# First layer of a graph network on turned node tiles, centred by means that go through DRAM

## What is computed

```
h = max(layernorm(x), 0)                      # no gain, no shift
def sage(x, Wp, bp, Wl, bl, Wr):
    p   = relu(x @ Wp.T + bp)
    agg = segment_sum(p[src], dst) / max(count(dst), 1)
    return agg @ Wl.T + bl + x @ Wr.T
def relu_ln(x, g, b):                          # relu, then layernorm with g and b
    ...
h = relu_ln(sage(h, layer 0), g0, be0)
h = relu_ln(sage(h, layer 1), g1, be1)
out = x + sage(h, layer 2)
```

## Time and profile before

| | us |
|---|---|
| median of 3 runs | 1519.19 |
| lowest and highest | 1514.76, 1520.58 |
| the profiled execution | 1518.14 |
| its span in the profile | 1516.4 |

### The profile page before, as it was taken

The page is one execution under the profiler, slowest core; times in us unless marked ns, Lnnn a source line. Parts: engine busy times, 40 slices in busy tenths (PEclk is TensorE's granted clock), DMA queues, the critical chain, the costliest instruction groups (busy, mean ns, idle before and its releaser), DMA issues.

```text
span 1516.4 us, 21038 instructions
## 1 busy us (share of the span) xinstructions
PE 1493.8 (99%) x7213; PEld 1216.6 (80%) x7213; DVE 970.3 (64%) x2084; ACT 682.8 (45%) x1267; POOL 604.6 (40%) x532
## 2 busy tenths in 40 slices
PE   7999999999999999999999999999999999999999
PEld 5788887888888888888788888888888777888887
DVE  7999875555555686766565555568766746555552
ACT  5545552332233676766223233356666732233221
POOL 4774355666523000100434432334464463444221
PEclk9999999999999999999999999999999999999999
DMA  8899875555544778786654555479999984554545
GB/s 304 313 347 318 287 260 181 119 85 91 95 85 56 257 268 306 266 284 241 197 111 85 91 91 90 54 249 343 381 349 356 367 279 95 91 90 84 94 59 146
DMA packets 157734, 298.14 MB, mean 197 GB/s; under 512 B 21565, under 2 KB 21756, under 8 KB 157500
## 3 DMA queue, kind: packets, MB, share of 16 engines
q1 hardware_dynamic: 127308, 231.17, 43.6%
q0 software_dynamic: 29744, 64.57, 24.7%
q10 hardware_dynamic: 576, 1.05, 0.2%
HBM read 136.54 MB, written 160.08 MB: 196 GB/s over the span
## 4 chain that ended last, share of the span: by engine, by line
PE 85%; DMA 5%; DVE 3%; issue 3%; POOL 2%; ACT 1%; SPq 1%; ACTq 0%; POOLq 0%
PE bank L750 11%; PE bank L751 11%; PE bank L752 11%; PE bank L738 9%; PE bank L842 7%; PE bank L840 7%; PE bank L841 7%; PE bank L821 7%; PE bank L820 7%; PE bank L819 7%; DMA residual<-x 3%; DMA node_x<-xn 1%; POOL residual L627 1%; DMA rows_in<-node_z 1%; ACT xn L957 1%
## 5 line engine op out<-in xcount | busy, mean ns | idle before, releaser
L750 PE MATMUL bank<-w_high,h_low 128*128 128x512 f32 x876 | 365.8, 418 | 0.0
L751 PE MATMUL bank<-w_low,h_high 128*128 128x512 f32 x876 | 346.6, 396 | 0.0
L752 PE MATMUL bank<-w_high,h_high 128*128 128x512 f32 x876 | 345.8, 395 | 0.0
L977 ACT ACTIVATE h_high<-h_pre 128x500 fp32r<-128x500 f32 x120 | 74.7, 622 | 448.9 <-DVE h_pre L1272 448.9
L609 POOL DMA_INDIRECT rows_in<-node_x,sorted_src x120 | 123.9, 1032 | 247.3 <-PE bank L738 169.3
L752 PEld LDWEIGHTS bank<-w_high,h_high 128*128 128x128 f32 x876 | 165.8, 189 | 39.9
L819 PE MATMUL bank<-xt_low,w_high 128*128 128x500 f32 x480 | 195.2, 407 | 1.7 <-issue 1.7
L957 ACT ACTIVATE xn<-rows_in,off,rstd 128x512 f32<-128x512 f32 x237 | 188.4, 804 | 15.0 <-issue 12.5
L840 PE MATMUL bank<-w_high,h_low 128*125 128x512 f32 x480 | 190.6, 397 | 1.0 <-DVE h_low L1278 1.0
L842 PE MATMUL bank<-w_high,h_high 128*125 128x512 f32 x480 | 190.0, 396 | 0.0
L751 PEld LDWEIGHTS bank<-w_low,h_high 128*128 128x128 f32 x876 | 165.9, 189 | 29.7
(11 more groups left out here) (114 smaller groups left out, 2251.1 us busy)
## 6 DMA issues: line engine op xcount, KB each, us to landing
node_x<-xn SPq DMA_DIRECT2D x237, 256.0 KB
rows_in<-node_z SPq DMA_DIRECT2D x158, 256.0 KB
node_z<-rows_out SPq DMA_DIRECT2D x142, 256.0 KB
out<-rows_out SPq DMA_DIRECT2D x79, 256.0 KB, 4.0
rows_in<-x SPq DMA_DIRECT2D x78, 256.0 KB
residual<-x SPq DMA_DIRECT2D x78, 256.0 KB, 5.0
rows_in<-node_x SPq DMA_DIRECT2D x24, 256.0 KB, 2.6
node_z<-bias_z SPq DMA_DIRECT2D x16, 256.0 KB
```

The source lines that it names most:

```text
L750: nc.tensor.matmul(psum, low[:, k, :], w_high("r", l)[:, k, :], start=(k == 0), stop=False)
L751: nc.tensor.matmul(psum, high[:, k, :], w_low("r", l)[:, k, :], start=False, stop=False)
L752: last = nc.tensor.matmul(psum, high[:, k, :], w_high("r", l)[:, k, :], start=False, stop=(k == K - 1))
```

## The change

Only layer 0 and the start of its edge stage are changed.

- **Turned loads.** The host gives x a second time as `x_t`, in which every node tile lies turned (feature by node). SyncE loads a tile of it straight into `xn` (ring of 4, 5 steps ahead of the product). The four transposes of each node tile are gone, and so is the store to `node_x` of layer 0.
- **Means.** In a turned tile a node is a column, so the mean must lie along the columns on every partition. For product tiles below 20 and for the late tiles ScalarE and VectorE write a diagonal of minus the means in a high and a low part (128x128), and TensorE multiplies both by ones (`spread_mean`, two matmuls of 128x128). From tile 20 on, the means of four tiles (`minus_mean`, 16 bytes on a partition) are stored to DRAM and loaded back to all partitions (2 KB each).
- **Centring.** VectorE adds them to the turned tile, in place (`centre`, 128x512). ScalarE writes the high part with relu from it, VectorE the low part. Both read SBUF where they read PSUM before. The tile is not divided.
- **Roots.** ScalarE keeps the root of each node (`spread`), VectorE inverts four tiles at once, and `node_out` of layer 0 multiplies by it while it adds the bias. `late_out` does so for late tiles.
- **Statistics** of a product tile stand 5 to 6 steps ahead at first, then two tiles in a step from step 3 to step 9, then 12 steps ahead, so that they end at step 58 (before, they ended later).
- **Edges.** Edge rows are gathered from x itself, so they are normalised after the gather: for each of 40 edge tiles `bn_stats`, `bn_aggr`, root, `rstd`, `off` and a ScalarE pass in place, from step 63 on and then beside the edge stage.
- **Ranks** are made by ScalarE (sign with a sum) in place of VectorE, and `rows_of` has one operation more. `edges_in_order` moves from step 54 to 58. GpSimd gathers the first 8 edge tiles before it spreads `carry`, and 12 columns of counts instead of 16 before the ninth tile. The counts stand 2.5 to a step from step 5, instead of 2 from step 3.
- At the end of layer 0 the late tiles get their means after each edge product, and layers 1 and 2 wait for the low part of the last late tile before they load rows.

```diff
+STATS = ((2, 6), (8, 5), (22, None), (None, 12))
+AHEAD_DIAG = 4
+AHEAD_SPREAD = 3
+AHEAD_SPLIT = 2
+BY_PE = 20
+EARLY = 2
+AHEAD_LOAD_T = 5
+DIAGS = 3
...
+COUNTS = 5
...
+STEP_COUNTED = 21
+STEP_SORTED = 58
+EARLY_COUNTS = 12
...
+STEP_EDGE_NORM = 63
...
+            def load_turned(t):
+                slot = t % XN_RING
+                if t >= XN_RING:
+                    sp.wait_ge(xt_low_done, node_no(0, t - XN_RING) + 1)
+                sp.dma_start(xn[:, slot, :], x_t[t * P:(t + 1) * P, :]).then_inc(t_loaded[slot], DMA)
...
+                    if l == 0 and XN_RING <= i + AHEAD_LOAD_T < product_count[0]:
+                        load_turned(i + AHEAD_LOAD_T)
+                    for g in means_at(i - 1) if l == 0 else ():
+                        sp.wait_ge(n_minus, unit_of[0][min(4 * g + 3, product_count[0] - 1)] + 1)
+                        sp.dma_start(mean_table[g], minus_mean[:, 4 * g:4 * g + 4]).then_inc(mean_stored, DMA)
+                    for g in means_at(i - 2) if l == 0 else ():
+                        sp.wait_ge(mean_stored, DMA * (g - BY_PE // 4 + 1))
+                        sp.wait_ge(rows_stored, DMA)
+                        if g - BY_PE // 4 >= 2:
+                            sp.wait_ge(n_centred, 4 * (g - 1))
+                        sp.dma_start(mean_rows[g % 2].rearrange("p m a -> p (m a)"),
+                                     mean_table[g:g + 1].rearrange("g p a -> g (p a)").to_broadcast([P, 4 * P])
+                                     ).then_inc(mean_loaded[g % 2], DMA)
...
+                    out=rows_in[:, slot, :], out_offset=None, in_=node_x if l else x_in,
...
+                    if l == 0 and t == IN_RING:
+                        spread_carry()
+                        pool.wait_ge(count_rows, 1)
+                        pool.wait_ge(counts_stored, DMA)
+                        for c in range(EARLY_COUNTS):
+                            gather_counts(c)
...
+                pe.wait_ge(n_diag_low, d + 1)
+                psum, slot = bank[c % 2][:, 0:P], d % DIAGS
+                nc.tensor.matmul(psum, ones_r[:], diag_low[:, slot, :], start=True, stop=False)
+                nc.tensor.matmul(psum, ones_r[:], diag_high[:, slot, :], start=False, stop=True).then_inc(turned, 1)
...
+            def first_xt_high(t):
+                act.wait_ge(n_centred, t + 1)
+                if t >= XT_RING:
+                    act.wait_ge(n_product, t - XT_RING + 1)
+                S.activation(node_xt(True, t), xn[:, t % XN_RING, :], ACT.Relu).then_inc(xt_high_done, 1)
...
+                S.activation(diag_high[:, slot, :], ident[:], ACT.Identity, scale=minus_mean[:, t:t + 1]
+                             ).then_inc(n_diag_high, 1)
...
+            def node_centre(t):
+                dve.wait_ge(t_loaded[t % XN_RING], DMA * turns(t, XN_RING))
+                if t < BY_PE:
+                    dve.wait_ge(turned, turn_value(node_no(0, t)))
+                    centre(xn[:, t % XN_RING, :], bank[t % 2][:, 0:P])
+                else:
+                    g = t // 4
+                    dve.wait_ge(mean_loaded[g % 2], DMA * ((g - BY_PE // 4) // 2 + 1))
+                    centre(xn[:, t % XN_RING, :], mean_rows[g % 2][:, :, t % 4])
...
+            def centre(rows, minus):
+                x = rows.rearrange("p (k m) -> p k m", k=K)
+                minus = minus.rearrange("p (a m) -> p a m", a=1).to_broadcast([P, K, P])
+                V.tensor_tensor(x, x, minus, ALU.add).then_inc(n_centred, 1)
...
+                    V.scalar_tensor_tensor(out=rows_out[:, slot, :], in0=bank[4 + t % 4][:],
+                                           scalar=spread[:, t:t + 1], in1=bias_z[:], op0=ALU.mult, op1=ALU.add
+                                           ).then_inc(n_out, 1)
...
+                    else:
+                        for u in first_units(i):
+                            first_stats(u)
+                        if is_product(l, i - 1):
+                            node_out(l, i - 1)
+                        for u in first_units(i):
+                            first_mean(u)
+                        for t in first_at(i, AHEAD_SPREAD):
+                            node_centre(t)
+                        for u in first_units(i):
+                            minus_of(u)
+                        for cols in scales_at(i):
+                            scale_of(cols)
+                        for t in first_at(i, AHEAD_SPLIT):
+                            node_xt_low(l, t)
+                        for t in first_at(i, AHEAD_DIAG):
+                            if t < BY_PE:
+                                diag_low_of(t)
+                        for k in R_CHUNKS.get(i, ()):
+                            low_of("r", 0, k)
+                        edge_statistics(edge_norms(i))
                     if l and i in LATE_OUT_AT:
                         late_out(l - 1, LATE - len(LATE_OUT_AT) + LATE_OUT_AT.index(i))
                     if l == 0 and i == STEP_ROWS_FLOAT:
                         keys_along_rows()
...
+                first_norms = range(2 * GROUP, 2 * GROUP + 2) if l == 0 else ()
+                edge_statistics(first_norms)
...
                 h_pre_of(l, 0, 0)
+                edge_factors(first_norms)
```

More of the change, by code:

```diff
@@ L311, in units_at @@
         def units_at(l, p):
-            units = []
-            for n in range(max(0, p - len(LATER)), min(p + 1, product_count[l])):
-                if n + (sum(n < c for c in LATER) if l == 0 else 0) == p:
-                    u = unit_of[l][n]
-                    units += [u] + ([u + 1] if u + 1 < NODE_TILES and tile_of[l][u + 1] >= product_count[l] else [])
-            return units
+            if not 0 <= p < product_count[l]:
+                return []
+            u = unit_of[l][p]
+            return [u] + ([u + 1] if u + 1 < NODE_TILES and tile_of[l][u + 1] >= product_count[l] else [])
@@ new lines, in first_at, with stats_step, stats_at @@
+        def first_at(i, ahead):
+            return [t for t in (i + ahead, i + ahead + 1) if 0 <= t < product_count[0]
+                    and t - ahead - (1 if t < EARLY else 0) == i]
+        def stats_step(t):
+            for until, ahead in STATS:
+                if until is None or t < until:
+                    return t - ahead if ahead else STATS[1][0] - STATS[1][1] + (t - STATS[1][0]) // 2
+        def stats_at(i):
+            return [t for t in range(product_count[0]) if stats_step(t) == i]
@@ new lines, in first_units, with scales_at, means_at @@
+        def first_units(i):
+            return [u for t in stats_at(i) for u in units_at(0, t)]
+        def scales_at(i):
+            last = product_count[0] - 1
+            found = [slice(t - t % 4, t + 1) for t in stats_at(i - 1) if t % 4 == 3 or t == last]
+            return found + ([slice(last + 1, NODE_TILES)] if last in stats_at(i - 1) else [])
+        def means_at(i):
+            last = product_count[0] - 1
+            return [t // 4 for t in stats_at(i) if t >= BY_PE and (t % 4 == 3 or t == last)]
@@ L320, in late_no, with edge_norms_beside, counts_at @@
+        def edge_norms_beside(s):
+            t = s + 2 * GROUP + 3
+            return [t - 1, t] if s == 0 else [t] if t < EDGE_TILES else []
+        def counts_at(i):
+            return [t for t in range(EDGE_TILES) if STEP_COUNT + 2 * t // COUNTS == i]
         def late_no(t):
@@ L879, in _ @@
                     edge_product(l, s)
+                    for j in late_turns(l, s) if l == 0 else ():
+                        late_turn(l, j)
                 if l + 1 < LAYERS:
@@ new lines, in rank @@
+            def rank(t):
+                g = t // GROUP
+                if t == 0:
+                    act.wait_ge(digits, 5)
+                else:
+                    act.wait_ge(placed, t)
+                act.wait_ge(row_loaded[t // (EDGE_TILES // ROW_CHUNKS)], DMA)
+                S.activation(unused[0:EDGE_ROWS, :],
+                             key_row[0:EDGE_ROWS, g * GROUP:(g + 1) * GROUP, :].rearrange("p a e -> p (a e)"),
+                             ACT.Sign, bias=key_f[0:EDGE_ROWS, t:t + 1], scale=-1.0,
+                             accum_out=place[0:EDGE_ROWS, t:t + 1]).then_inc(placed, 1)
@@ L1014, in _ @@
                     edge_xt_high(l, t)
+                for t in range(2 * GROUP, 2 * GROUP + 2) if l == 0 else ():
+                    std_of(t % IN_RING, t)
+                for t in range(2 * GROUP, 2 * GROUP + 2) if l == 0 else ():
+                    edge_norm(t)
                 for m in range(GROUP):
@@ L1059, in late_out, with late_centre, scale_of @@
+            def late_centre(j):
+                c = late_no_of(0, j)
+                dve.wait_ge(late_loaded[j], DMA)
+                dve.wait_ge(turned, turn_value(c))
+                centre(rows_in[:, j, :], bank[c % 2][:, 0:P])
+            def scale_of(cols):
+                dve.wait_ge(n_root, max(unit_of[0][t] for t in range(cols.start, cols.stop)) + 1)
```

(1 more changed line is left out.)

374 lines of the change are left out of this document (254 added, 120 removed).

## The result

The changed kernel takes 1544.37 us (median of 4 runs, 1542.50 to 1547.21), the kernel before on the same chip 1517.38. The ratio is **1.0180** (95% interval 1.0167 to 1.0193): slower by 27 us, and 4 us beyond the upper end of the range. The profiled execution has a span of 1542.8 us against 1516.4.

A forecast was written before the change was run, and what follows sets the result against it. VectorE becomes the bound before step 59; -5.1 us to the first edge product, +0.3 for late tiles and +7.5 for costs bounded from afar make +2.7 on 1518.14: 1521 us, own range 1512 to 1527, 8 in 10 within 1502 to 1540.

The forecast's parts named there:

- The bound: Layer 0's node stage: VectorE, 2.84 us a step on average, becomes the bound above TensorE's 2.80, until step 59.
- what rows bounded only from afar: VectorE before step 59: turned loads 3 us, means through DRAM 1, GpSimd beside VectorE 2, masks and spreads 1.5; together +7.5.
- the centring (two inputs of 512, 0.60 as its neighbours): VectorE's new addition of the means to each turned tile in a node step: 0.60 us, like neighbouring operations.
- rival 3: From tile 20 on, centring reads means at every fourth word: 0.28 us each, 14 us over 51 tiles, 1535; chance 0.13.
- GpSimd beside VectorE: Low part and centring, with two SBUF inputs, slow down beside GpSimd work such as Wl's split: 2 us, ends 0 and 4.
- Loads and means: Late turned loads 3 us for steps 1 to 9 (0 to 15); SyncE's wait for the means' store 1 us (0 to 13).
- Rival 2: Node steps: turned loads' landing sets the step, 15 us more, up to 25 with means' waits; 1530 to 1545; chance 0.22.
- The small operations: VectorE's small operations in a plain node step, among them `minus_mean`: 0.12 and 0.13 us.
- Late tiles: Late tiles lose eight turns (3.4 us), get sixteen short matmuls (1.8 to 3.7) and two waits of about 0.7: +0.3.
- The first steps and the masks: VectorE ends step 9 at 58.3 us; masks and spreads on steps 5 to 20 add 1.5 us, ends 0 and 4.
- Edge rows' statistics hidden: Edge stage: 0.92 us more a tile on VectorE and two ScalarE passes, beside about 6 us of TensorE's work, cost nothing.
- The path to the first edge product: GpSimd's gathers after edges in order at 210.5 us hold VectorE; first edge product at 261.4 us, -5.1 against today.

The follow-up runs named there:

- run 2: Changed kernel, but from tile 20 on the centring reads its means at steps of 1, 2, 3 or 4 words by tile (values wrong): 1542.65 us, single run.
- run 4: Changed kernel with means read at neighbouring words (values wrong) and the four low halves of Wl made by VectorE: 1531.04 us, ratio 1.0089.
- run 5: run 4, but from tile 20 on a turned load brings one row of 128 (values wrong): 1514.91 us, ratio 1.0050.
- run 6: run 4, but the means' load reads weights of the same size, without waiting for the means' store (values wrong): 1523.32 us in a single run, ratio 1.0096.
- run 1: Changed kernel, but from tile 20 on the centring reads its means as 128 neighbouring words (values wrong): 1538.8 us, ratio 1.0139.
- run 3: Changed kernel, but the four low halves of layer 0's Wl are made by VectorE in steps 48 to 51, not GpSimd: 1541.88 us, ratio 1.0165.
- run 7: run 3, but all 71 tiles' means are spread by TensorE, none through DRAM: 1527.38 us, ratio 1.0134.
- run 9: run 3, but means are stored by pairs of tiles, 256 pieces of 8 bytes, and every second word is read: 1551.12 us, ratio 1.0271.
- run 11: run 3 with the strided read, but turned loads of one row instead of 128 from tile 20 on (values wrong): 1529.21 us, ratio 1.0128.
- run 10: run 3, but ScalarE turns each four means into dense rows, and late tiles' diagonals come one edge tile earlier: 1528.25 us, ratio 1.0120.
- run 8: run 4 with true values, means stored turned in 512 pieces of 4 bytes so they come back dense: 1598.18 us, ratio 1.0605.

## Why the prediction was wrong

**The bound** was right: VectorE full, TensorE with gaps. **The sum** was wrong. By the prediction's own stations (step ends on VectorE, us):

| | forecast | measured | excess of the stretch |
|---|---|---|---|
| end of step -1 | 18.0 | 19.7 | +1.7 |
| end of step 9 | 58.3 | 59.6 | -0.4 |
| end of step 20 | 93.3 | 98.5 | +3.9 |
| end of step 58 | 207.2 | 229.8 | +17.4 |
| first edge product | 261.4 | 290.4 | +6.4 |
| from there to the end | 1250.2 | 1252.4 | +2.2 |

The forecast put 7.5 us on top for what rows bounded only from afar; 23.7 us are missing beyond them.

- **The step that failed is "the centring (two inputs of 512, 0.60 as its neighbours)".** With dense means it is 0.58 from start to start, with the table's means 0.97: 51 x 0.37 = 19 us over the forecast, 4 in the third stretch's steps, 38 in the fourth's, 9 in the fifth's. I had seen it and made it rival 3, with a chance of 0.13 and a price of 0.28 us from a difference of 22 ns between two operations of 40 elements. The price was too low (0.28 where it is 0.40), and the chance was far too low: run 2 shows the cost in each of its twelve reads at every fourth word. Rival 3 is what happened. Its time, 1535, was short by the terms below.
- **GpSimd beside VectorE**, 2 us with an end at 4: it was 5.4 in one piece. The earlier trace rows showed one addition of 1.28 us holding one operation; four in a row held one operation for all four, and the TensorE behind it.
- **Loads and means**, 3 + 1 us: 10.8 us of VectorE's waits for turned loads in after. Within the ends given, but elsewhere: 1.3 us in steps 1 to 9, where I had them, and 9.5 from tile 20 on. Rival 2 was true as a mechanism, but masked by the strided read; runs 4 to 6 lay it bare. The means' way through DRAM by itself cost nothing that run 6 could show.
- **The small operations** were taken as 0.12 and 0.13 and are 0.09 and 0.06. In steps 21 to 58 all that is neither centring nor wait takes 85.8 us, where the forecast has 91.1: -5.3, which hid part of the miss. So the stretch's 17.4 us are 14.1 of strided read, 5.4 behind GpSimd and 3.3 of waits for loads, less 5.3.
- **Late tiles**, +0.3: it was 1.3. "Two waits of about 0.7" became three gaps of 0.92 to 1.00 and 2.9 us of idle TensorE, since ScalarE makes the diagonals behind a high half and an edge tile's output in its own order.
- **The first steps and the masks** were right: 0.4 us off over steps 0 to 9.
- **Edge rows' statistics hidden:** right in the edge stage from 307 us on (TensorE 30.00 of 30 us). At its start the wait of 1.06 us for ScalarE's pass is most of 1.2 us that the forecast put at nothing. In steps 63 to 67, where I had TensorE as the bound at 2.80, VectorE needs 3.86 us a step: 5.3 us in five steps, most of the fifth stretch's 6.4.
- **The path to the first edge product** was forecast as GpSimd's chain of gathers, with VectorE waiting for the ninth and tenth edge tile. In after it takes their statistics at 276.85 us without a wait, so VectorE's own work is the path. The forecast's 210.5 us for edges in order also stands 3.3 us behind its own end of step 58 without a reason; in after the first gather starts at 228.63, before that step ends.

What stays open: run 5 has its first edge product at 263.6 us, where the kernel before has it at 266.5, and yet is slower by 0.5% (6.1 us). Most of that is the chip. The only trace of before is from the first group's, where it took 1518.1 us, and on run 5's it took 1508.8. From the first edge product to the end after and runs 1 to 4 take 1252.4 to 1254.1 us, runs 5, 6, 7, 9 and 11, on the other two chips, 1246.2 to 1247.5. So, as an estimate, 5 to 6 of the 9.4 us between the chips lie behind the first edge product and 3 to 4 ahead of it, and the kernel before would have it at some 263 us on run 5's chip: run 5 is not ahead there, and loses 2.5 us behind it. The other 2.5 us are how far its profiled execution (1512.46) lies below its median. Without a trace of before on that chip this is not shown.

## What to carry over

Before an operand is laid out for a cheap store, price its read on the engine that will be the bound: count how many of the words read share 16 bytes, and take the ratio from an operation of full length. Where a change frees one engine, write down the second limit behind the new bound as well, since the cure of the first uncovers it (here 21 us of read gave back 12 us of waits for loads). And a rival that a known rule supports deserves more than a tenth of the chance.

## What the runs showed of the hardware

- VectorE, fp32 from SBUF, 512 elements, second input at 4, 8, 12, 16 bytes: 0.66, 0.66, 0.84, 1.07 us. ScalarE's copy of such rows at every fourth word: 1.13 us, where its other operations on 512 dense elements from SBUF take some 0.62 (run 10).
- A store of 2 KB from SBUF to DRAM on SyncE's queue, as 256 pieces of 8 bytes and as 512 of 4: 7.8 and 11.3 us from issue to landing (runs 9 and 8); as 128 of 16, half or more landed within 3.9 us (run 3). That makes 14 ns for each piece more in the second doubling, by the waits 11, and at least 30 in the first. The Trainium skill, "DMA: Bandwidth & Descriptors", section "Measured (HBM→SBUF, 128 partitions, SWDGE, issued from GpSimd)", has about 10.5 ns a packet behind its floor for the smallest loads. The second doubling is near that; the first is not.
- In after, a VectorE operation with two SBUF inputs was listed 0.55 us ahead of GpSimd's first addition (206.25 and 206.80) and still ended only 0.93 us after the last of four, 6.42 us long where its kind takes 1.07. In 1 and 2 one took 4.80 and 5.77 us beside the same four. That an operation that starts first also goes first can't be read from these rows; the starts on GpSimd are rough.
